# The first three steps of an attention turn: transposes ahead of the first scores on TensorE, bank emptying first on VectorE

## The chip, the cores and the metric

The kernel runs on one core of a Trainium2 chip, in one launch. The metric is the device time of that launch in microseconds (us), lower being better; a comparison takes the median of several runs. One further execution was recorded by the hardware profiler, and all rows below are from it.

## The reference

One transformer layer on an input of 2 sequences, 1024 tokens, 512 features, all in float32:

```python
q = (x @ Wq.T)                       # 32 heads of 128, rotary embedding applied
c_kv = x @ Wdk.T                     # latent of 512
k = mix(rope(x @ Wkr.T), c_kv @ Wupk.T)   # 8 key heads
v = c_kv @ Wupv.T                    # 8 value heads
scores = where(causal, q @ k.T / sqrt(128), -1e9)
out = softmax(scores) @ v            # every key head serves 4 query heads
x = layernorm(x + out @ Wo.T)
x = layernorm(x + W2 @ (silu(W1 @ x) * (W3 @ x)))   # W1, W2, W3 unpacked from 4 bits
```

## The kernel before

**Precision.** Each float32 operand of a large product is split into a rounded part HI and a remainder LO, and each product is made as three matmuls, HI·HI, HI·LO and LO·HI (`three_pass`, L255). So every tile that leaves TensorE and enters a product again is first copied by ScalarE (the HI part) and then subtracted by VectorE (the LO part).

**Stages.** Stage A makes latents, keys and values of all tokens (the first scores start at 232.8 us of the trace). Then come 16 turns of attention, one for each pair of a sequence and a key head (`turn_of`, called by `turns` at L404: a first turn, a loop of turns 1 to 14, a last turn 15, and a short tail called "end"). The feed-forward stage follows. The change touches the turns alone.

**A turn** has 32 steps. A step is one cell: 128 queries (tile i = c // 4) of one query head (h = c % 4) against the keys that they may see. Cells are pipelined over the steps:

- step s: TensorE makes the scores of cell s (`scores`, L1047, into `b_sps`); VectorE takes mask and maximum (`mask_max`, L902) and ScalarE the exponential with its sum (`exp`, L742).
- step s+2: VectorE takes the reciprocal of the sum (`reciprocal`, L911), ScalarE multiplies by it (`normalise`, L749).
- step s+3 (`LAG`): TensorE transposes the weights, in one or two pieces of up to four 128x128 tiles (`transposes`, L1062, into `b_tps`); ScalarE copies a piece to HI (`hi_pt`, L755), VectorE makes LO (`lo_pt`, L916).

Between these TensorE works off a queue of "fill" products by a table (`FILL`, `ROOM`): query projections of a coming half (`q0`, `q1`), weights times values (`pv`), and the output projection (`wo`). A fill product that is finished in step s is taken from its bank by ScalarE and VectorE in step s+1 (`take`): for a query `swap_q` (L715) and `cos_q` (L884), for a `pv` `hi_ot` (L771) and `lo_ot` (L927), for a `wo` `add_y` (L932). One step later still come the second half of the rotary embedding (`add_q`, L891, VectorE), its HI part (`hi_q`, L722, ScalarE) and its LO part (`split_q`, GpSimd).

**What sets the order.** Every engine runs its own list, in order. Within a step the order of the jobs is a tuple of `ACT_ORDER`, `DVE_ORDER` or `PE_ORDER`, the first tuple in steps 0 to 2 (`part_of`, L94). In step 0 TensorE first does all fill of that step, in the loop the 21 matmuls of `pv` tile 6 of the turn before. ScalarE's order in steps 0 to 2, not changed, is: take, first piece, q, normalise, second piece, exp.

**At a turn's start** the three pipelines overlap. Step 0 holds: scores of cell 0 of the new turn, transposes of cell 29 of the turn before, `reciprocal` and `normalise` of cell 30, `cos_q` of the new turn's fourth query head. Step 1 holds: scores of cell 1, transposes of cell 30, `reciprocal` and `normalise` of cell 31, `hi_ot` and `lo_ot` of `pv` tile 6, `add_q` and `hi_q` of the fourth head, and the first 8 matmuls of `wo` tile 5, which go to the bank that `cos_q` empties. Step 2 transposes cell 31. The new turn's keys come by four DMAs that SyncE issues once the last scores of the turn before are made, since there is one key buffer:

```python
if step == 0 and turn in ("loop", "last"):
    sp.wait_ge(s_done, CELLS * it)
    load_k(it)
```

Of the kernel before, what the change touches and what calls it, by code (L numbers as in the profile page):

```python
# [54 lines left out]
def pieces(c):  # L55

    i = c // GQ
    first = c if i < 4 else 16 + 2 * (c - 16)
    out = [(first, 0, min(4, i + 1))]
    if i >= 4:  # L60
        out.append((first + 1, 4, i - 3))
    return out
# [31 lines left out]
def part_of(step):  # L94

    return (step >= LAG) + (step >= 16) + (step >= 24)
# [6 lines left out]
             ("take", "q", "normalise", 0, "exp", 1, "weights"),  # L103
             ("take", "normalise", 0, "exp", "weights", 1, "q"),
             ("take", "normalise", 0, "exp", "weights", 1, "q"))
DVE_ORDER = (("q", "max", "take", 0, 1),
             ("q", "max", "take", 0, 1),
             ("take", "q", "max", 0, 1),
             ("take", "max", "q", 0, 1))
PE_ORDER = (("scores", "fill", "fill", 0, "fill", 1),  # L110
            ("fill", "scores", 0, "fill", "fill", 1),
            ("scores", "fill", 0, "fill", 1, "fill"),
            ("scores", "fill", 0, "fill", 1, "fill"))
# [59 lines left out]
def plan_of(turn):  # L173
    return FIRST if turn == "first" else LOOP
# [9 lines left out]
def cut(parts, weights):  # L184

    total, shares = sum(b - a for _n, a, b in parts), []
    ends = [round(total * sum(weights[:k]) / sum(weights)) for k in range(len(weights) + 1)]
    for lo, hi in zip(ends, ends[1:]):
        at, share = 0, []
        for place, a, b in parts:  # L190
            x, y = max(lo, at), min(hi, at + b - a)
            if x < y:
                share.append((place, a + x - at, a + y - at))
            at += b - a
        shares.append(share)
    return shares
# [68 lines left out]
def attention(nc, x, xT, wqT, wkrT, wdkT, wupkT, wupvT, woT, cosT, sinT, xs_d, k_d, v_d, y_d):  # L265


    with ExitStack() as ctx:
# [112 lines left out]
        def cell_at(step, it, turn):  # L381

            if step >= 0:
                return (it, step) if turn != "end" and step < CELLS else None
            return (it - 1, step + CELLS) if turn != "first" else None
# [444 lines left out]
        def _(dve):  # L830
# [116 lines left out]
            def turn_of(it, turn):  # L947
                for step in steps_of(turn):
                    here = cell_at(step, it, turn)
                    for job in DVE_ORDER[part_of(step)]:  # L950
                        if job == "take":
# [47 lines left out]
        def _(pe):  # L999
# [47 lines left out]
            def scores(it, c):  # L1047
                i, h = c // GQ, c % GQ
                if c == 0 and type(it) is int and it == 0:
                    pe.wait_ge(a_bank_free, a_count(END, VG + V_LATE - 1) + a_FREE0)  # L1050
                if c == 0:
                    pe.wait_ge(k_in, 64 * (it + 1))
                pe.wait_ge(q_lo, 8 * it + 4 * (i // 4) + h + 1 + QLO0)
                pe.wait_ge(sc_done, CELLS * it + c + 1)
                if c in (16, 17):
                    pe.wait_ge(ot_lo, QT * it + c - 16 + 1)
                q = (i % 4) * P
                for k, (a, b) in enumerate(scores_width(i)):
                    last = three_pass(nc, sps[c % 2][:, 512 * k:512 * k + b - a],
                                      [(lambda p: qs[:, i // 4, h, p, q:q + P], lambda p: kt[:, p, a:b])])  # L1060
                last.then_inc(s_done, 1)

            def transposes(it, c, piece):
                n, j0, nj = piece
                pe.wait_ge(norm_done, CELLS * it + c + 1)
                pe.wait_ge(pt_lo, PIECES * it + n + 1)
                for j in range(nj):
                    last = nc.tensor.transpose(tps[n % 2][:, j], sc[:, c % S_RING, (j0 + j) * P:(j0 + j + 1) * P],  # L1068
                                               ident[:])
                last.then_inc(t_done, 1)  # L1070
# [54 lines left out]
            def fill(it, turn, parts):  # L1125
                for n, a, b in parts:
                    if not valid(n, turn):
                        continue
                    kind, t, g, _s = plan_of(turn).fill[n]
                    bk = plan_of(turn).bank[n]  # L1130
                    if a == 0 and bk < 2 and (before := bank_before(n, turn)):
                        bank_taken(before[0], before[1], it + before[2])
                    elif a == 0 and bk < 2:
                        pe.wait_ge(q_cos, GQ - 1 + n)
                    if kind == "pv":
                        values(it + g, t, bk, a, b)
                    elif kind == "wo":
                        project(it + g, t, bk, a, b)
                    elif kind == "va":
                        late_values(t, bk, a, b)  # L1140
                    else:
                        queries(it + g, int(kind == "q1"), t, bk, a, b)

            def turn_of(it, turn):
                for step in range(CELLS):
                    parts = plan_of(turn).spread[step]
                    here, cell = cell_at(step, it, turn), cell_at(step - LAG, it, turn)
                    if step == 0:
                        fill(it, turn, parts)
                        parts = []  # L1150
                    ts = pieces(cell[1]) if cell else []
                    shares = cut(parts, SHARES[len(ts)])
                    for job in PE_ORDER[part_of(step)]:
                        if job == "scores":
                            if here:
                                scores(*here)
                        elif job == "fill":
                            if shares:
                                fill(it, turn, shares.pop(0))
                        elif job < len(ts):  # L1160
                            transposes(*cell, ts[job])
# [16 lines left out]
            for h in range(GQ):  # L1178
# [3 lines left out]
                if h < V_LATE:  # L1182
                    a_group(END, VG + h, a_values(h))
            turns(pe, turn_of)


# [535 lines left out]
```

## Time and profile before

| | us |
|---|---|
| median of 3 runs | 2485.4 |
| lowest and highest of them | 2484.12 and 2489.93 |
| the profiled execution | 2487.67 |
| its span, first to last instruction | 2485.9 |
| TensorE busy with matmuls in the span | 2408.9 (97%) |
| ScalarE busy | 1597.1 (64%) |
| VectorE busy | 1425.2 (57%) |
| GpSimd busy | 571.6 (23%) |

The profiled execution took 1.8 us more than its span. Its mean granted TensorE clock is 0.991 of the full one. The ends of matmul records are modelled, so that TensorE's real occupation is better read from the distance between starts. L12 is line 12 of the kernel. A row that stands for several instructions tells the first start and the time that all were busy; the bracket tells how long the engine was idle ahead of the first one, and what released it. In rows PE is TensorE, PEld its loading of weights (it runs beside the matmuls), DVE VectorE, ACT ScalarE.

### The profile page before, as it was taken

Reading aid. Unit: us, or ns where it says so; the run is one execution under the profiler, and the core shown is the slowest. Engines: PE = TensorE matmul, PEld = TensorE weight load, DVE = VectorE, ACT = ScalarE, POOL = GpSimd, SP = SyncE. Lnnn points to the kernel's source line nnn. Section 1 sums busy time; section 2 is a strip of 40 time slices with the busy share of each in tenths; the row PEclk is TensorE's granted clock in tenths of the full one; section 3 lists DMA queues with packets and bytes.
Section 4 is the critical chain, followed back from the end, with each engine's and each line's share of the span. In section 5 each row is a group of like instructions: output and inputs, shape, how many; then the busy total and the mean of one; then the engine's idle time right before and its main releaser. Section 6 shows DMA issues by size and latency. Waiting matters only on the chain. (4 is left out here: it accounts for less than half of the span.)

```text
span 2485.9 us, 40420 instructions
## 1 busy us (share of the span) xinstructions
PE 2408.9 (97%) x12028; PEld 1997.4 (80%) x12028; DVE 1425.2 (57%) x3333; ACT 1597.1 (64%) x3213; POOL 571.6 (23%) x445
## 2 busy tenths in 40 slices
PE   8999999999999999999999999999999996899998
PEld 7887888888888888888888888888888875678886
DVE  4334656566666666566666666666666666842332
ACT  4223878787777878787777878787877762332211
POOL 3002313223231323132222313231322202300000
PEclk9999999999999999999999999999999998999999
DMA  7767333324242323233242424232332316520100
GB/s 266 276 217 272 124 98 111 114 93 155 67 155 82 131 82 133 93 110 115 96 156 72 148 80 132 90 124 93 110 122 89 116 42 190 153 78 34 51 34 17
DMA packets 110979, 293.38 MB, mean 118 GB/s; under 512 B 10832, under 2 KB 27728, under 8 KB 101648
## 3 DMA queue, kind: packets, MB, share of 16 engines
q1 hardware_dynamic: 110928, 292.73, 35.4%
q8 instruction: 28, 0.46, 0.1%
q14 instruction: 23, 0.19, 0.0%
HBM read 208.80 MB, written 88.08 MB: 119 GB/s over the span
## 5 line engine op out<-in xcount | busy, mean ns | idle before, releaser
L924 DVE TENSOR_TENSOR b_pt<-b_tps,b_pt 128x512 fp32r<-128x512 f32 (+3 forms) x768 | 427.1, 556 | 370.7 <-ACT b_pt L767 369.6
L752 ACT ACTIVATE b_sc<-b_sc,b_rinv 128x896 f32<-128x896 f32 (+7 forms) x512 | 397.0, 775 | 294.4 <-DVE b_rinv L914 290.9
L260 PE MATMUL b_sps<-b_kt,b_qs 128*128 128x512 f32 (+4 forms) x2304 | 501.8, 344 | 10.2 <-DMA b_kt<-k_d 10.1
L260 PEld LDWEIGHTS b_sps<-b_kt,b_qs 128*128 128x128 f32 x2304 | 403.0, 188 | 72.4 <-issue 18.9
L260 PE MATMUL b_ps<-b_xs,b_wq 128*128 128x512 f32 x1536 | 442.3, 407 | 2.6 <-issue 2.6
L260 PE MATMUL b_ps<-b_pt,b_vt 128*128 128x512 f32 x1584 | 436.4, 402 | 2.5 <-DVE b_ys L935 2.5
L260 PE MATMUL b_ps<-b_wo,b_ot 128*128 128x512 f32 x1536 | 423.7, 406 | 1.8 <-DVE b_ys L935 0.6
L767 ACT ACTIVATE b_pt<-b_tps 128x512 fp32r<-128x512 f32 (+3 forms) x768 | 364.5, 475 | 63.7 <-PE b_tps L1068 63.0
L746 ACT ACTIVATE b_sc<-b_sc,b_nmax 128x896 f32<-128x896 f32 (+7 forms) x512 | 392.7, 767 | 1.0 <-DVE b_nmax L906 1.0
L1068 PE MATMUL b_tps<-b_ident,b_sc 128*128 128x128 f32 x2304 | 377.4, 274 | 8.9 <-DVE b_pt L924 5.7
L906 DVE CUSTOM_DVE_ANT_0 b_sc<-b_sps,b_mask 128x896 f32<-128x896 f32 (+7 forms) x512 | 380.2, 743 | 0.0
L1068 PEld LDWEIGHTS b_tps<-b_ident,b_sc 128*128 128x128 f32 x2304 | 287.7, 140 | 97.3 <-DVE b_pt L924 15.8
L260 PEld LDWEIGHTS b_ps<-b_pt,b_vt 128*128 128x128 f32 x1584 | 285.8, 189 | 50.8 <-DVE b_ys L935 2.9
L260 PEld LDWEIGHTS b_ps<-b_xs,b_wq 128*128 128x128 f32 x1536 | 275.1, 190 | 47.7 <-issue 3.0
L260 PEld LDWEIGHTS b_ps<-b_wo,b_ot 128*128 128x128 f32 x1536 | 270.7, 189 | 48.4 <-DVE b_qf L888 4.1
L598 POOL TENSOR_TENSOR b_sw<-b_sw,b_sin 128x512 f32<-128x512 f32 x128 | 165.5, 1293 | 498.5 <-ACT b_sw L720 498.5
L602 POOL TENSOR_TENSOR b_qs<-b_qf,b_qs 128x512 fp32r<-128x512 f32 x124 | 160.3, 1293 | 482.3 <-ACT b_qs L726 482.3
L914 DVE RECIPROCAL b_rinv<-b_rsum 128x1 f32<-128x1 f32 x512 | 81.1, 158 | 194.5 <-PE b_sps L260 182.9
L888 DVE TENSOR_TENSOR b_qf<-b_ps,b_cos 128x512 f32<-128x512 f32 x128 | 88.5, 691 | 98.2 <-ACT b_sw L720 54.2
L260 PE MATMUL c_a<-c_xs,c_w 128*128 (+3 forms) x528 | 135.3, 407 | 8.4 <-DVE c_hb L1508 4.2
L611 POOL TENSOR_TENSOR b_wo<-b_wraw,b_wo 128x512 fp32r<-128x512 f32 x64 | 83.0, 1297 | 239.7 <-ACT b_wo L740 239.7
L1616 PE MATMUL c_y<-c_w,c_hs 128*128 128x512 f32 (+1 forms) x528 | 129.6, 395 | 7.1 <-DVE c_hs L1514 7.1
(137 smaller groups left out, 2386.9 us busy)
## 6 DMA issues: line engine op xcount, KB each, us to landing
b_xs<-xs_d SPq DMA_DIRECT2D x32, 2048.0 KB, 9.1
b_ys<-y_d SPq DMA_DIRECT2D x128, 256.0 KB, 2.7
y_d<-b_ys SPq DMA_DIRECT2D x128, 256.0 KB, 2.5
k_d<-a_ks SPq DMA_DIRECT2D x32, 512.0 KB, 4.2
v_d<-a_vs SPq DMA_DIRECT2D x32, 512.0 KB, 3.0
b_kt<-k_d SPq DMA_DIRECT2D x64, 256.0 KB, 4.5
b_vt<-v_d SPq DMA_DIRECT2D x16, 1024.0 KB, 4.8
b_wraw<-in_wqT SPq DMA_DIRECT2D x64, 256.0 KB, 2.7
```

The lines of the kernel that those rows point to most:

```text
L260: ins = nc.tensor.matmul(out, *every[n], start=(n == 0), stop=(n == len(every) - 1))
L598: nc.gpsimd.tensor_tensor(sw[:], sw[:], sinq[:, blk * TB:blk * TB + TB], ALU.mult).then_inc(sin_done, 1)
L602: nc.gpsimd.tensor_tensor(qs[:, blk, h, LO], qf[:], qs[:, blk, h, HI], ALU.subtract).then_inc(q_lo, 1)
L611: nc.gpsimd.tensor_tensor(wo[:, h, LO], wraw[:, h % 2], wo[:, h, HI], ALU.subtract).then_inc(w_lo, 1)
L746: nc.scalar.activation(sc[:, slot, 0:w], sc[:, slot, 0:w], ACT.Exp, bias=nmax[:, slot:slot + 1], scale=-1.0, accum_out=rsum[:, slot:slot + ...
L752: nc.scalar.activation(sc[:, slot, 0:w], sc[:, slot, 0:w], ACT.Copy, scale=rinv[:, slot:slot + 1])\
L767: nc.scalar.activation(pt[:, u % PT_UNITS, HI, 0:nj, h * P:(h + 1) * P], tps[n % 2][:, 0:nj], ACT.Copy)\
L888: nc.vector.tensor_tensor(qf[:], banks[bk], cosq[:, blk * TB:blk * TB + TB], ALU.mult)\
L906: nc.vector.tensor_tensor_reduce(out=like_banks(sc[:, slot, 0:w], i), in0=both_banks(sps[c % 2], i), in1=like_banks(mask[:, S - w:S], i), ...
L924: nc.vector.tensor_tensor(pt[:, u, LO, 0:nj, h * P:(h + 1) * P], tps[n % 2][:, 0:nj], pt[:, u, HI, 0:nj, h * P:(h + 1) * P], ALU.subtract) ...
L1068: last = nc.tensor.transpose(tps[n % 2][:, j], sc[:, c % S_RING, (j0 + j) * P:(j0 + j + 1) * P], ident[:])
L1616: last = nc.tensor.matmul(yps[t][:], hs[0:w, f % 2, a, t * P:(t + 1) * P], w2[0:w, b, f], start=(f == 0 and k == 0), stop=(f == FT - 1 and ...
```

## The change

Two edits. In step 0 TensorE makes both pieces of transposes, and then the scores. In steps 0 to 2 VectorE does "take" first, then "q", then "max" (which holds the wait for the scores, the reciprocal of an earlier cell, and mask and maximum).

```diff
-DVE_ORDER = (("q", "max", "take", 0, 1),
+DVE_ORDER = (("take", "q", "max", 0, 1),
              ("q", "max", "take", 0, 1),
              ("take", "q", "max", 0, 1),
              ("take", "max", "q", 0, 1))
...
-                    for job in PE_ORDER[part_of(step)]:
+                    for job in (0, 1, "scores") if step == 0 else PE_ORDER[part_of(step)]:
                         if job == "scores":
                             if here:
                                 scores(*here)
```

The lists of ScalarE, GpSimd and SyncE stay as they are. TensorE's list in the loop, from the 21 fill matmuls of step 0 on (b_sps is written by scores, b_tps by transposes):

```order
 L260 MATMUL b_ps<-b_pt,b_vt 128x512 x21
+L1065 ISA
+L1066 REGISTER_ALU
+L1068 MATMUL b_tps<-b_ident,b_sc 128x128 x4
+L1066 REGISTER_ALU
+L1068 MATMUL b_tps<-b_ident,b_sc 128x128 x4
 L1052 ISA
 L1053 ISA
 L1054 ISA
 L260 MATMUL b_sps<-b_kt,b_qs 128x256 x3
```

The eight transposes of cell 29, with their waits, now stand ahead of the waits and the three matmuls of the first scores; before, they stood behind them.

VectorE's list in the loop, step 0, before (b_qf is `cos_q`, b_rinv the reciprocal, L906 mask and maximum, b_pt `lo_pt`):

```order
L914 RECIPROCAL b_rinv<-b_rsum 128x1
L906 ISA b_sc,b_nmax<-b_sps,b_mask 128x128
L906 ISA b_nmax 128x1
L886 ISA
L888 TENSOR_TENSOR b_qf<-b_ps,b_cos 128x512
L920 ISA
L924 TENSOR_TENSOR b_pt<-b_tps,b_pt 128x4x128
```

and now:

```order
L888 TENSOR_TENSOR b_qf<-b_ps,b_cos 128x512
L899 ISA
L900 ISA
L913 ISA
L914 RECIPROCAL b_rinv<-b_rsum 128x1
L906 ISA b_sc,b_nmax<-b_sps,b_mask 128x128
L906 ISA b_nmax 128x1
L920 ISA
L924 TENSOR_TENSOR b_pt<-b_tps,b_pt 128x4x128
```

`cos_q` moved from behind the maximum to the front, ahead of the wait for the scores (L899).

VectorE's list in the loop, step 1, before (the first b_qf row is `add_q`, b_ot is `lo_ot`):

```order
L895 TENSOR_TENSOR b_qf<-b_qf,b_sw 128x512
L899 REGISTER_ALU
L900 REGISTER_ALU
L913 REGISTER_ALU
L914 RECIPROCAL b_rinv<-b_rsum 128x1
L906 ISA b_sc,b_nmax<-b_sps,b_mask 128x128
L906 ISA b_nmax 128x1
L928 ISA
L929 TENSOR_TENSOR b_ot<-b_ps,b_ot 128x512
```

and now:

```order
L928 ISA
L929 TENSOR_TENSOR b_ot<-b_ps,b_ot 128x512
L895 TENSOR_TENSOR b_qf<-b_qf,b_sw 128x512
L899 REGISTER_ALU
L900 REGISTER_ALU
L913 REGISTER_ALU
L914 RECIPROCAL b_rinv<-b_rsum 128x1
L906 ISA b_sc,b_nmax<-b_sps,b_mask 128x128
L906 ISA b_nmax 128x1
```

`lo_ot`, with its wait for ScalarE's `hi_ot` (L928), moved ahead of `add_q` and of the reciprocal.

## Rows read from the trace of the kernel before

**Rows 1.** The page's part 1: busy time, share of the span and instructions by engine.

```profile
PE 2408.9 (97%) x12028; PEld 1997.4 (80%) x12028; DVE 1425.2 (57%) x3333; ACT 1597.1 (64%) x3213; POOL 571.6 (23%) x445
```

**Rows 2.** TensorE's waits over the whole span: total us, times, longest.

```profile
PE b_sps L260 <- DMA b_kt<-k_d: 10.1, 14, 1.0
...
PE b_tps L1068 <- DVE b_pt L924: 5.7, 20, 0.6
```

**Rows 3.** Timeline of one turn's start, TensorE: start us, us, engine line op [idle before <-releaser].

```profile
452.74 4.94 PE L260 MATMUL b_ps<-b_pt,b_vt 128*128 128x512 f32 x21
...
458.27 0.61 PE L260 MATMUL b_sps<-b_kt,b_qs 128*128 128x256 f32 x3 [0.59 <-DMA b_kt<-k_d]
...
458.72 1.04 PE L1068 MATMUL b_tps<-b_ident,b_sc 128*128 128x128 f32 x8
...
459.52 0.60 PE L260 MATMUL b_sps<-b_kt,b_qs 128*128 128x256 f32 x3
...
460.20 1.24 PEld L260 LDWEIGHTS b_ps<-b_wo,b_ot 128*128 128x128 f32 x6 [0.29 <-DVE b_qf L888]
...
461.73 0.60 PE L1068 MATMUL b_tps<-b_ident,b_sc 128*128 128x128 f32 x4
...
464.64 0.51 PEld L1068 LDWEIGHTS b_tps<-b_ident,b_sc 128*128 128x128 f32 x4
464.79 0.60 PE L1068 MATMUL b_tps<-b_ident,b_sc 128*128 128x128 f32 x4
```

**Rows 4.** The same timeline, ScalarE.

```profile
459.36 0.60 ACT L767 ACTIVATE b_pt<-b_tps 128x512 fp32r<-128x512 f32 x1 [3.62 <-PE b_tps L1068]
...
459.86 1.14 ACT L752 ACTIVATE b_sc<-b_sc,b_rinv 128x1024 f32<-128x1024 f32 x1
...
460.90 0.59 ACT L767 ACTIVATE b_pt<-b_tps 128x512 fp32r<-128x512 f32 x1
...
461.76 0.59 ACT L774 ACTIVATE b_ot<-b_ps 128x512 fp32r<-128x512 f32 x1
...
462.36 0.60 ACT L767 ACTIVATE b_pt<-b_tps 128x512 fp32r<-128x512 f32 x1
...
462.86 0.62 ACT L726 ACTIVATE b_qs<-b_qf 128x512 fp32r<-128x512 f32 x1
...
463.38 1.14 ACT L752 ACTIVATE b_sc<-b_sc,b_rinv 128x1024 f32<-128x1024 f32 x1
```

**Rows 5.** The same timeline, VectorE.

```profile
459.13 0.16 DVE L914 RECIPROCAL b_rinv<-b_rsum 128x1 f32<-128x1 f32 x1 [3.91 <-PE b_sps L260]
...
461.52 0.69 DVE L924 TENSOR_TENSOR b_pt<-b_tps,b_pt 128x512 fp32r<-128x512 f32 x1 [0.77 <-ACT b_pt L767]
...
462.12 0.68 DVE L895 TENSOR_TENSOR b_qf<-b_qf,b_sw 128x512 f32<-128x512 f32 x1
...
462.72 0.15 DVE L914 RECIPROCAL b_rinv<-b_rsum 128x1 f32<-128x1 f32 x1
...
462.99 0.68 DVE L929 TENSOR_TENSOR b_ot<-b_ps,b_ot 128x512 fp32r<-128x512 f32 x1
```

**Rows 6.** The same timeline, two pairs of a releaser and an idle ScalarE.

```profile
451.06 0.16 DVE L914 RECIPROCAL b_rinv<-b_rsum 128x1 f32<-128x1 f32 x1
...
451.26 1.15 ACT L752 ACTIVATE b_sc<-b_sc,b_rinv 128x1024 f32<-128x1024 f32 x1 [1.04 <-DVE b_rinv L914]
...
472.96 0.69 DVE L895 TENSOR_TENSOR b_qf<-b_qf,b_sw 128x512 f32<-128x512 f32 x1 [0.48 <-POOL b_sw L598]
...
473.68 0.63 ACT L726 ACTIVATE b_qs<-b_qf 128x512 fp32r<-128x512 f32 x1 [1.05 <-DVE b_qf L895]
```

**Rows 7.** Timeline of the last turn's start, TensorE.

```profile
1933.79 1.52 PE L260 MATMUL b_ps<-b_pt,b_vt 128*128 128x512 f32 x6
...
1935.39 0.62 PE L260 MATMUL b_sps<-b_kt,b_qs 128*128 128x256 f32 x3
```

**Rows 8.** Timeline behind the last turn, TensorE alone.

```profile
2045.00 0.63 PE L1068 MATMUL b_tps<-b_ident,b_sc 128*128 128x128 f32 x4 [0.50 <-DVE b_pt L924]
```

## Prediction

> **What bounds the kernel now.** I read the page's busy shares first: TensorE 97%, no other engine over 64% [rows 1]. So time can only be won where TensorE stands still, or lost by making it stand still. Next TensorE's waits. The largest entry inside the attention turns is the first scores of a turn waiting for the keys: 10.1 us in 14 waits, 0.72 us each, one in each of the 14 turns of the loop; the second is transposes waiting for VectorE's `lo_pt`, 5.7 us in 20 [rows 2]. Then the timeline of one turn's start on three engines. TensorE starts its 21 fill matmuls at 452.74. They cost 0.2275 us each (the row's 4.94 less the modelled 0.39 of the last, over 20), so TensorE is free at 457.52; the first scores start at 458.27, when the keys are there, and the transposes that the keys have nothing to do with stand behind them, from 458.72 [rows 3]. A second small wait follows: the six `wo` matmuls start at 460.20, their weights having waited 0.29 for `cos_q`, which stood behind the maximum [rows 3]. The reader is to see one more thing: ScalarE is idle for 3.62 us before 459.36 and then has ten or so operations without a gap up to `normalise` at 463.38 [rows 4], and the transposes of step 2 at 464.79 need the result of that one [rows 3].
>
> **What goes away.** The eight transposes take 458.72 to 459.52, 0.80 us, and 0.80 is more than the 0.75 between 457.52 and 458.27 [rows 3]. So they start at 457.52, the scores at about 458.31 instead of 458.27, the second scores (0.44 later) at 458.75 instead of 459.52. `cos_q` now runs in VectorE's idle 3.91 us [rows 5]: what it needs from ScalarE was done by 455.74, which is 459.36 less 3.62 [rows 4]. The `wo` matmuls can then start when the second scores are issued, at 459.10 instead of 460.20: TensorE is 1.1 us ahead there. If that lasted, 15 turns by 1.1 would be 16.5 us.
>
> **What it costs: the chain that the scores start.** In step 0 VectorE's reciprocal of cell 30 stands behind the wait for the scores, in both kernels, and ScalarE's list hangs on it. The scores come 0.04 later, so nothing behind them on that path comes earlier by TensorE's 1.1 us. I follow it with distances between starts.
>
> 1. Reciprocal of cell 30: 458.27 to 459.13 is 0.86 [rows 3, 5]; now 458.31 + 0.86 = 459.17.
> 2. `normalise` of cell 30: an idle ScalarE starts 0.20 behind a reciprocal (451.06, 451.26) [rows 6]; now 459.37. Before 459.86, because ScalarE was at the first piece's copy from 459.36 [rows 4]; that copy now comes over a microsecond sooner. This is all that ScalarE wins: 0.49.
> 3. Copy of the second piece 1.04 later, at 460.41, `hi_ot` 0.86 after that, at 461.27 (before 460.90 and 461.76) [rows 4].
> 4. VectorE: the second `lo_pt` at 460.41 + 0.62 = 461.03 (before 460.90 to 461.52 [rows 4, 5]), free again 0.60 later at 461.63. Then comes the moved `lo_ot`, which waits for `hi_ot`: with the same 0.62, 461.89. It stood at 462.99 before, when its input had been ready for long [rows 5].
> 5. `add_q` is now behind it: 461.89 + 0.60 = 462.49, before 462.12 [rows 5]. The wait for `hi_ot` is thus added in front of `add_q`, and behind `add_q` in VectorE's queue are the reciprocal of cell 31, the second maximum and the next `lo_pt`; only the first matters, since it goes from 462.72 to 463.09, still ahead of its use.
> 6. `hi_q`: 0.72 after `add_q` with ScalarE idle (472.96, 473.68) [rows 6]: 463.21, before 462.86, when ScalarE reached it straight from the copy at 462.36 [rows 4]. ScalarE now stands idle there.
> 7. `normalise` of cell 31: 0.52 later, 463.73, before 463.38. It lasts 1.14 [rows 4], so it ends at 464.87 instead of 464.52, and the weights of the step 2 transposes are loaded 0.12 after (before: 464.64) [rows 3], at 464.99.
> 8. TensorE pays for a restart after a wait. The six `wo` matmuls, which had waited, take 1.53 to the next start, 460.20 to 461.73, against 6 x 0.2275 = 1.37: 0.16 [rows 3]. Transposes are not shown restarting, so their price lies between 0 and 0.16; loads and matmuls of theirs are half as long, and I take 0.05. The transposes run at 465.04 instead of 464.79.
>
> So in a turn of the loop TensorE is 1.1 us ahead at the `wo` matmuls and 0.25 us behind at the transposes of step 2. Its own work would have brought it there at 459.10 + (464.79 - 460.20) = 463.69; it gives back about 0.2 at the transposes of cell 30 (loaded at 459.37 + 1.14 + 0.12 = 460.63, where TensorE would be at 459.10 + 1.37 = 460.47), another 0.2 at their second piece, which waits for the `lo_pt` at 461.03, and some 0.9 at step 2. What follows in the turn hangs on TensorE and on the same chain, and is late by the same quarter of a microsecond; the next turn's keys are asked for after the last scores, so nothing gives it back.
>
> **The sum.**
> - 14 turns of the loop, 0.25 each: 3.5 us. Bounds: 0.15 and 0.45 (step 8 at 0 and each of the eight steps a hundredth shorter; step 8 at 0.16 and half of that again at the second piece, whose `lo_pt` hangs on the same `normalise`).
> - Turns whose keys come earlier than here: the scores then wait for the transposes instead. The mean wait is 0.72, here it is 0.59 by the page's count; that costs at most 0.15 where it is shorter, and I take 0.3 us for all, between 0 and 1.
> - The last turn: the fill ends at 1933.79 + 6 x 0.2275 = 1935.15 and the scores start at 1935.39 [rows 7], 0.24 later and not 0.75. The transposes' 0.80 moves them by 0.55, and the chain behind moves along: 0.7, between 0.4 and 0.9.
> - Behind the last turn there are no scores, but `lo_ot` stands ahead of the last reciprocal, by one distance of 0.60 [rows 5]; the transposes there already wait 0.50 for VectorE [rows 8], so the chain decides there too. 0.6, between 0 and 0.6.
> - The first turn makes no transposes in step 0; the emptied bank ahead of the maximum delays one exponential, which step 3's transposes use much later: 0, between -0.3 and 0.3.
> - Instructions added or removed: none of any weight. No DMA moves past another.
>
> Together 3.5 + 0.3 + 0.7 + 0.6 = 5.1 us: from the profiled execution's 2487.67 to 2492.8. That execution lies 2.3 above the median of the three runs, 2485.4; from the median I get 2490.5, 0.2% slower. A measurement of this kernel tells about 0.3%, 7.5 us, from no change, so most of this counts as the same.
>
> One rule speaks against my result. The row shows a wait of 0.59 for the keys ahead of work that does not need them [rows 3]. The Trainium skill, DMA: Bandwidth & Descriptors, section Rules for kernel authors, says to issue a DMA early, do compute, and wait on its semaphore late; by it the 10.1 us of [rows 2] would be the gain. The trace agrees that the wait can be covered, not that its end is what decides step 2.
>
> **Rivals.**
> - *The wait's removal shows in the time (faster).* If `hi_q` or the `normalise` behind it can run when they did before, TensorE keeps at least the wait: 10.1 us, to 2475.3, and with the `cos_q` wait up to 16.5, to 2469. For it: the largest wait inside the turns goes. Against: step 5, where `add_q` has an input that did not exist before, and step 2, by which ScalarE gets only 0.49. Chance 0.13.
> - *The chain's cost is paid more than once (slower).* Three groups of transposes hang on the late `normalise`: step 2's first, its second, and cell 0's in step 3. In the forecast the second and third are late with the first. If a restart costs the full 0.16, the first pays 0.11 more than I took; and if one more of them restarts from a wait of its own, another 0.11. A turn then costs 0.25 + 2 x 0.11 = 0.47, so 6.6 + 1.6 = 8.2 us: 2493.6, over the bound. It decides once the second piece's `lo_pt` ends later than TensorE gets to it; by the distances above it ends at 463.73 + 1.04 + 0.62 + 0.69 = 466.08, within 0.1 of that point. For it: the transposes already wait for `lo_pt` 20 times [rows 2]. Against: those waits are 0.28 on average. With the last turn and the keys at their ends it reaches 2497. Chance 0.20.
> - *The order does not do what it says.* If TensorE cannot start the transposes at 457.52, because the bank pair or the weights of cell 29 are late, nothing moves on TensorE, and the late scores stay. Their weights were normalised from 451.26 on [rows 6], six microseconds before. Then 0 to +2 us, 2486. Chance 0.05, within the same.
>
> **How the numbers follow.** Forecast 0.62, faster rival 0.13, slower rival 0.20, no effect 0.05. Faster by over 0.3%: 0.13; slower by over 0.3%: 0.20 (the slower rival's part over the bound, and a little of the forecast's upper end in exchange for its lower part); same: 0.67. The likeliest case alone spans 2487 to 2493. The range is 2478 to 2496: it leaves out most of the faster rival and the last of the slower one.
>
> **What would show it.** Right: the wait for the keys gone from TensorE's list or under 2 us; the first scores of a turn still about 0.2 us behind the keys' landing; in its place about 14 waits of transposes for ScalarE's `normalise`, 0.7 to 1.1 us each, some 13 us; VectorE's `add_q` 4.2 us after the turn's first scores instead of 3.85; ScalarE idle ahead of `hi_q`; step 2's transposes 6.7 us after those scores instead of 6.52. Wrong: if those transposes come 6.5 us or less after the first scores, the chain of steps 4 to 7 was shorter than I have it, and the time falls below 2485; if TensorE's sum of waits grows by over 10 us, the slower rival holds.

## The result, and the profile after

| | before | changed |
|---|---|---|
| median of 18 runs each, us | 2487.41 | 2493.59 |
| lowest and highest | 2482.83, 2491.27 | 2486.35, 2496.09 |
| span of the profiled execution | 2485.9 | 2492.1 |

The ratio is 1.0024, with a 95% interval of 1.0017 to 1.0031: 4.2 to 7.7 us slower, clear of zero and within what I had called the same. Forecast were +5.1 us. One run of the kernel before, among those that e5 to e7 below are held against, took 2976.7 us at a granted clock of 0.749 instead of 0.99 and is left out of every figure.

The page's first line shows nothing of it: TensorE is busy to the same 97% as in [rows 1].

```profile
PE 2415.9 (97%) x12028; PEld 1995.6 (80%) x12028; DVE 1427.4 (57%) x3333; ACT 1599.1 (64%) x3213; POOL 571.9 (23%) x445
```

TensorE's waits over the span show where the time went (total us, times, longest). They answer to [rows 2].

```profile
PE b_tps L1068 <- ACT b_sc L752: 15.1, 30, 0.9
...
PE b_tps L1068 <- DVE b_pt L924: 5.7, 19, 0.6
...
PE b_sps L260 <- DMA b_kt<-k_d: 1.2, 3, 0.6
```

The wait for the keys is down from 10.1 us to 1.2, as intended. The keys have not lost their say, though: in 11 of the loop's 14 turns the scores still start 0.21 to 0.22 us behind the landing of the last key transfer, as before; what is gone is the idle time ahead of them, now filled with transposes. In its place stand transposes that wait for ScalarE's `normalise`, 15.1 us; before, that pair had 1.2 us in 8.

The start of the loop's third turn in the changed kernel, TensorE, in the columns of [rows 3]:

```profile
572.04 1.04 PE L1068 MATMUL b_tps<-b_ident,b_sc 128*128 128x128 f32 x8
...
573.08 0.97 PE L260 MATMUL b_sps<-b_kt,b_qs 128*128 128x256 f32 x6
...
573.89 1.55 PE L260 MATMUL b_ps<-b_wo,b_ot 128*128 128x512 f32 x6
...
575.42 0.65 PE L1068 MATMUL b_tps<-b_ident,b_sc 128*128 128x128 f32 x4
...
576.55 0.66 PE L1068 MATMUL b_tps<-b_ident,b_sc 128*128 128x128 f32 x4
...
579.79 0.42 PEld L1068 LDWEIGHTS b_tps<-b_ident,b_sc 128*128 128x128 f32 x4 [1.27 <-DVE b_pt L924]
579.80 0.65 PE L1068 MATMUL b_tps<-b_ident,b_sc 128*128 128x128 f32 x4 [0.86 <-ACT b_sc L752]
```

The transposes come first, the scores follow at 573.08 without idle time ahead of them, and the six `wo` matmuls start 0.81 behind the scores instead of 1.93. Then every group of transposes in steps 1 and 2 restarts from a wait (in the trace the loads of their weights stood idle 0.41, 0.44, 1.27 and 0.22 ahead of the four groups), and the first of step 2, at 579.80, has waited 0.86. It starts 6.72 behind the first scores; before it was 464.79 - 458.27 = 6.52 [rows 3].

ScalarE in the same stretch, to be held against [rows 4]:

```profile
572.68 0.60 ACT L767 ACTIVATE b_pt<-b_tps 128x512 fp32r<-128x512 f32 x1 [2.42 <-PE b_tps L1068]
...
574.14 1.15 ACT L752 ACTIVATE b_sc<-b_sc,b_rinv 128x1024 f32<-128x1024 f32 x1 [0.87 <-DVE b_rinv L914]
...
576.06 0.58 ACT L774 ACTIVATE b_ot<-b_ps 128x512 fp32r<-128x512 f32 x1
...
578.00 0.63 ACT L726 ACTIVATE b_qs<-b_qf 128x512 fp32r<-128x512 f32 x1 [0.87 <-DVE b_qf L895]
...
578.54 1.13 ACT L752 ACTIVATE b_sc<-b_sc,b_rinv 128x1024 f32<-128x1024 f32 x1
```

Its first copy comes early and then it is idle, first 0.87 for the reciprocal, later 0.87 for `add_q`. Before, it had no gap between these operations. VectorE, against [rows 5]:

```profile
573.95 0.16 DVE L914 RECIPROCAL b_rinv<-b_rsum 128x1 f32<-128x1 f32 x1 [2.96 <-PE b_sps L260]
...
576.67 0.69 DVE L929 TENSOR_TENSOR b_ot<-b_ps,b_ot 128x512 fp32r<-128x512 f32 x1 [0.18 <-ACT b_ot L774]
...
577.28 0.68 DVE L895 TENSOR_TENSOR b_qf<-b_qf,b_sw 128x512 f32<-128x512 f32 x1
...
577.88 0.16 DVE L914 RECIPROCAL b_rinv<-b_rsum 128x1 f32<-128x1 f32 x1
```

`lo_ot` waits for `hi_ot` (idle 0.18), and `add_q` comes at 577.28, 4.20 behind the first scores; before, 462.12 - 458.27 = 3.85.

The period of a turn splits into three parts. These are means over the 14 turns of the loop, from the starts in the two traces, in us:

| | before | changed | difference |
|---|---|---|---|
| keys asked for, until the first scores | 7.106 | 7.231 | +0.125 |
| of that, until the keys have landed | 6.887 | 6.997 | +0.110 |
| first scores, until the transposes of step 2 | 6.514 | 6.715 | +0.201 |
| those transposes, until the next keys are asked for | 100.030 | 100.041 | +0.011 |
| a whole turn | 113.649 | 113.987 | +0.338 |

14 x 0.338 = 4.7 of the spans' 6.2 us. The second line is the transfer itself; in the seven other kernels below its mean lay between 6.79 and 6.96 whatever they changed, and here three of the 14 turns (7.65, 7.37 and 7.35, the others 6.64 to 7.05) make the 7.00. So I take its 0.11 (1.5 us in the sum) for scatter of one execution; with one trace of each kernel that is not shown. The granted clock was 1.00 from 260 to 1929 us in both traces, so it has no part in the turns' difference. In the last turn the scores come 0.56 and the transposes another 0.12 later. The first turn, from its first scores to the request for the next keys, is 0.08 shorter, 104.53 instead of 104.61. Behind the last turn, in the changed kernel (TensorE):

```profile
2043.95 1.03 PE L1068 MATMUL b_tps<-b_ident,b_sc 128*128 128x128 f32 x8
...
2050.63 0.63 PE L1068 MATMUL b_tps<-b_ident,b_sc 128*128 128x128 f32 x4 [0.64 <-DVE b_pt L924]
2053.27 3.35 PE L260 MATMUL b_ps<-b_pt,b_vt 128*128 128x512 f32 x7 [2.01 <-DVE b_ys L935]
```

and before:

```profile
2038.87 1.03 PE L1068 MATMUL b_tps<-b_ident,b_sc 128*128 128x128 f32 x8
...
2047.63 1.67 PE L260 MATMUL b_ps<-b_pt,b_vt 128*128 128x512 f32 x6 [2.01 <-DVE b_ys L935]
```

From the first transposes to the restart of the `pv` matmuls it is 9.32 instead of 8.76, 0.56 longer. These parts make 5.9 of the 6.2 us; the rest, under 0.4, lies in stages that the change does not touch.

### The profile page after: what moved, and what is told of

Same layout as the page of the kernel before. It is cut to its first block and busy times, and to the rows that moved or that the text cites. A ratio compares the mean times of both kernels' runs of the same rounds, so it can differ in the third digit from the quotient of the medians.

```text
span 2492.1 us, 40420 instructions
## 1 busy us (share of the span) xinstructions
PE 2415.9 (97%) x12028; PEld 1995.6 (80%) x12028; DVE 1427.4 (57%) x3333; ACT 1599.1 (64%) x3213; POOL 571.9 (23%) x445
## 5 line engine op out<-in xcount | busy, mean ns | idle before, releaser
L260 PE MATMUL b_ps<-b_pt,b_vt 128*128 128x512 f32 x1584 | 437.8, 404 | 2.5 <-DVE b_ys L935 2.5
L1068 PE MATMUL b_tps<-b_ident,b_sc 128*128 128x128 f32 x2304 | 379.8, 275 | 22.0 <-ACT b_sc L752 15.1
L906 DVE CUSTOM_DVE_ANT_0 b_sc<-b_sps,b_mask 128x896 f32<-128x896 f32 (+7 forms) x512 | 380.4, 743 | 0.0
```

The lines of the kernel that those rows point to most:

```text
L260: ins = nc.tensor.matmul(out, *every[n], start=(n == 0), stop=(n == len(every) - 1))
L906: nc.vector.tensor_tensor_reduce(out=like_banks(sc[:, slot, 0:w], i), in0=both_banks(sps[c % 2], i), in1=like_banks(mask[:, S - w:S], i), ...
```

## Experiments

All seven were compared with the kernel before. The first four shared 15 runs of it (median 2486.88), the last three 27 (median 2485.91). The distances in the text are from the third turn, those in the table means over the 14 turns of the loop. The turns tell more than the whole times, since stages that no edit touches vary from trace to trace: the first scores start at 231.1 to 233.8 us, and from the restart of `pv` behind the last turn to the end it is 437.8 to 440.8.

| | scores to `add_q` | to `normalise` of cell 31 | to step 2's transposes | a turn | ratio to before, 95% |
|---|---|---|---|---|---|
| before | 3.85 | 5.10 | 6.51 | 113.65 | |
| changed | 4.20 | 5.45 | 6.72 | 113.99 | 1.0024 (1.0017 to 1.0031) |
| e1 TensorE's order alone | 3.33 | 5.07 | 6.50 | 113.55 | 0.9995 (0.9986 to 1.0004) |
| e2 VectorE's order alone | 4.72 | 5.97 | 7.23 | 114.22 | 1.0039 (1.0025 to 1.0052) |
| e3 take first in step 0 only | 3.33 | 4.59 | 5.90 | 112.95 | 0.9965 (0.9952 to 0.9979) |
| e4 e3 and early reciprocal | 2.53 | 3.86 | 5.38 | 112.41 | 0.9932 (0.9919 to 0.9946) |
| e5 changed and early reciprocal | 3.42 | 4.67 | 5.99 | 112.98 | 0.9975 (0.9966 to 0.9984) |
| e6 e4 with TensorE's old order | 3.86 | 5.11 | 6.38 | 113.50 | 0.9995 (0.9987 to 1.0004) |
| e7 e3, `lo_ot` behind `add_q` | 3.33 | 4.72 | 6.00 | 113.04 | 0.9977 (0.9968 to 0.9985) |

**e1.** The second hunk of the change alone; `DVE_ORDER` as before.

```diff
-                    for job in PE_ORDER[part_of(step)]:
+                    for job in (0, 1, "scores") if step == 0 else PE_ORDER[part_of(step)]:
```

> TensorE's half of the change alone: transposes ahead of the first scores in step 0, VectorE's order as before. Theory (the chain add_q, hi_q, normalise of cell 31 decides step 2, and only the moved lo_ot makes it late): the wait for the keys goes from TensorE's list, but the 0.7 to 0.9 us come back as a wait of the wo matmuls for cos_q, which still stands behind the maximum. add_q stays about 3.4 to 3.9 us and step 2's transposes about 6.5 us behind the turn's first scores. Time: +0.04 us a turn and 0.6 in the last turn, 0 to +2 us, same. Rival (making the scores wait behind the transposes is what costs): step 2's transposes 6.7 us behind the scores, +4 to +6 us. Third (the wait for the keys was the price): -10 us.

Measured: 2486.43 us against 2486.88, no difference. TensorE, third turn:

```profile
571.86 0.97 PE L260 MATMUL b_sps<-b_kt,b_qs 128*128 128x256 f32 x6
...
573.79 1.66 PE L260 MATMUL b_ps<-b_wo,b_ot 128*128 128x512 f32 x6 [0.96 <-DVE b_qf L888]
...
578.39 0.60 PE L1068 MATMUL b_tps<-b_ident,b_sc 128*128 128x128 f32 x4
```

The wait for the keys is gone and stands again, somewhat longer (14.1 us in 15 waits over the span), in front of the `wo` matmuls, released by `cos_q` behind the maximum. The transposes of step 2 start 6.53 behind the scores. So the transposes' precedence alone neither costs nor gains.

**e2.** The first hunk alone.

```diff
-DVE_ORDER = (("q", "max", "take", 0, 1),
+DVE_ORDER = (("take", "q", "max", 0, 1),
```

> VectorE's half alone: take, q, max in steps 0 to 2, TensorE's order as before. Theory: hi_ot comes only at 3.49 us behind the first scores as before, lo_ot 0.62 later, add_q at 4.71 (before 3.85), hi_q 5.43, normalise of cell 31 at 5.95 (before 5.10), step 2's transposes at 7.25 instead of 6.51: +0.74 us a turn, with 0.6 in the last turn and 0.6 behind it +11.5 us, 0.4 to 0.5 percent slower. Rival (the emptying of the bank for wo is what matters, the 0.29 us wait goes): -4 us. Rival (TensorE's order carries the loss): 0.

Measured: 2496.95 us, ratio 1.0039, 6 to 13 us slower. TensorE's scores, VectorE's `add_q`, TensorE's transposes of step 2:

```profile
572.66 0.62 PE L260 MATMUL b_sps<-b_kt,b_qs 128*128 128x256 f32 x3 [1.12 <-DMA b_kt<-k_d]
...
577.38 0.68 DVE L895 TENSOR_TENSOR b_qf<-b_qf,b_sw 128x512 f32<-128x512 f32 x1
...
579.90 0.65 PE L1068 MATMUL b_tps<-b_ident,b_sc 128*128 128x128 f32 x4 [0.84 <-ACT b_sc L752]
```

4.72 and 7.24 where 4.71 and 7.25 were expected. By the turns VectorE's new order alone costs more than the whole change, 7.23 against 6.72 from scores to transposes: the two hunks work against each other. The medians go the same way, but the intervals of the two ratios overlap.

**e3.** Both engines as changed in step 0, VectorE as before in steps 1 and 2 (`DVE_ORDER` not edited).

```diff
-                    for job in DVE_ORDER[part_of(step)]:
+                    for job in ("take", "q", "max", 0, 1) if step == 0 else DVE_ORDER[part_of(step)]:
...
-                    for job in PE_ORDER[part_of(step)]:
+                    for job in (0, 1, "scores") if step == 0 else PE_ORDER[part_of(step)]:
```

> The change as it is in step 0 on both engines, but VectorE's steps 1 and 2 in the order of before (q, max, take), so that add_q no longer waits behind lo_ot. Theory: add_q 3.3 us behind the first scores instead of 4.2, normalise of cell 31 at 4.6, step 2's transposes 5.9 us behind the first scores: 0.6 us a turn faster than before, -8 us against before and -14 against the changed kernel. Rival (the late scores or the landing of the keys carry the loss, not lo_ot): no faster than before, +3 to +6 us.

Measured: 2477.81 us, ratio 0.9965: about 9 us faster than before. The same three points:

```profile
567.76 0.96 PE L260 MATMUL b_sps<-b_kt,b_qs 128*128 128x256 f32 x6
...
571.08 0.68 DVE L895 TENSOR_TENSOR b_qf<-b_qf,b_sw 128x512 f32<-128x512 f32 x1
...
573.61 0.66 PE L1068 MATMUL b_tps<-b_ident,b_sc 128*128 128x128 f32 x4
```

3.32 and 5.85. The only difference to the changed kernel in the loop is where `lo_ot` stands in step 1 (in step 2 nothing is taken), and it turns 6 us lost into 9 won. The rival (late scores or late keys carry the loss) falls: the scores stand behind the transposes as in the changed kernel, and the keys, which landed after 6.82 us in the mean instead of 7.00, make at most 0.17 of the 1.03 us that a turn is shorter.

**e4.** e3, and in step 0 the reciprocal ahead of the wait for the scores.

```diff
+                            cell = cell_at(step - 2, it, turn)
+                            if cell and step == 0:
+                                reciprocal(*cell)
                             if here:
                                 scores_there(*here)
-                            if cell := cell_at(step - 2, it, turn):
+                            if cell and step > 0:
                                 reciprocal(*cell)
                             elif here:
                                 nc.vector.memset(spare[:, step:step + 1], 0.0)
```

> As the kernel with take first in step 0 only, and in step 0 the reciprocal of cell 30 also stands ahead of VectorE's wait for the scores (a tiny memset takes that wait). Theory: ScalarE's normalise of cell 30 no longer hangs on the scores, the whole list of ScalarE starts about 0.7 us earlier, and TensorE keeps the whole 1.1 us of a turn: step 2's transposes 5.4 us behind the first scores, -15 us against before (2472 to 2474). Rival (VectorE's wait for the scores is not on the path, TensorE's own work is): same time as without this edit.

Measured: 2469.84 us, ratio 0.9932, 17 us faster than before; no kernel here is faster. Scores, ScalarE's `normalise` of cell 30, `add_q`, transposes of step 2:

```profile
568.22 0.97 PE L260 MATMUL b_sps<-b_kt,b_qs 128*128 128x256 f32 x6
568.55 1.15 ACT L752 ACTIVATE b_sc<-b_sc,b_rinv 128x1024 f32<-128x1024 f32 x1
...
570.82 0.68 DVE L895 TENSOR_TENSOR b_qf<-b_qf,b_sw 128x512 f32<-128x512 f32 x1
...
573.49 0.60 PE L1071 MATMUL b_tps<-b_ident,b_sc 128*128 128x128 f32 x4
```

`normalise` of cell 30 starts 0.33 behind the scores instead of 1.06, and the transposes of step 2 follow the matmuls before them without a wait, 5.27 behind the scores. That is TensorE's own work: the chain is off the path. Twelve of the 14 turns have 5.25 to 5.30. In the other two a different wait shows, that for the DMA of the next block's inputs (`b_xs`), which delays the query products ahead of those transposes: in the first turn TensorE waits 0.95 us for it and the transposes come at 6.48, in the fourth at 5.50. In e3 it is the first turn alone (0.57 us of waiting, 6.57; the others 5.84 to 5.87). The means of the table, 5.38 and 5.90, contain these turns. The first turn of e4, whose scores start at 342.56:

```profile
348.48 0.73 PE L260 MATMUL b_ps<-b_xs,b_wq 128*128 128x512 f32 x2 [0.95 <-DMA b_xs<-xs_d]
...
349.04 0.60 PE L1071 MATMUL b_tps<-b_ident,b_sc 128*128 128x128 f32 x4
```

**e5.** The changed kernel with e4's edit of the reciprocal.

> The changed kernel, lo_ot still ahead of add_q, and in step 0 the reciprocal of cell 30 ahead of VectorE's wait for the scores. Theory (the chain that lo_ot lengthens starts at the scores only because the reciprocal hangs on them): ScalarE's normalise, hi_ot and so lo_ot come 0.7 us earlier, add_q 3.5 us behind the first scores instead of 4.2, step 2's transposes 6.0 instead of 6.7: 0.7 us a turn better than the changed kernel, -4 to -6 us against before. Rival (lo_ot costs by its place alone, wherever ScalarE is): as the changed kernel, +6.

Measured: 2480.12 us, ratio 0.9975, 6 us faster than before and some 12 faster than the changed kernel.

```profile
571.59 0.96 PE L260 MATMUL b_sps<-b_kt,b_qs 128*128 128x256 f32 x6
...
575.06 0.68 DVE L895 TENSOR_TENSOR b_qf<-b_qf,b_sw 128x512 f32<-128x512 f32 x1
...
577.58 0.65 PE L1071 MATMUL b_tps<-b_ident,b_sc 128*128 128x128 f32 x4 [0.58 <-ACT b_sc L752]
```

`add_q` still comes behind `lo_ot`, now 3.47 behind the scores, the transposes 5.99. The price of `lo_ot`'s place depends on when ScalarE gets to `hi_ot`, which is what the theory says. Against e4, whose order differs by `lo_ot`'s place, it still costs 0.61 us a turn in the means, and 0.66 without the turns that wait for `b_xs` (here the first, with 1.18 us of waiting and 6.71 from scores to transposes). The 14 turns of the trace are 9.4 us shorter than before, more than the 6 of the whole time; behind the last turn 0.56 is lost as in the changed kernel, and the stages that no edit touches took 3.4 us longer in this trace.

**e6.** e4 without the hunk on TensorE's order.

> VectorE as in the kernel with the early reciprocal and take first in step 0 only, TensorE's order as before. Theory: with the transposes behind the scores ScalarE's first copy of the turn comes at 459.4 as before, so the early reciprocal is of no use, and TensorE keeps its wait for the keys; only the 0.29 us wait of the wo matmuls goes, and step 2's transposes then wait a little for normalise: -0.1 us a turn, 0 to -3 us. Rival (the early reciprocal and the early cos_q carry the 17 us that the kernel with both orders won): -10 us or more.

Measured: 2484.93 us, ratio 0.9995, no difference that can be told. The mean distance to step 2's transposes fell by 0.14 as expected, 2 us in the sum. Early reciprocal and early `cos_q` are worth almost nothing as long as the transposes stand behind the scores.

**e7.** e3 with `lo_ot` behind `add_q` but ahead of the reciprocal of cell 31.

```diff
-DVE_ORDER = (("q", "max", "take", 0, 1),
+DVE_ORDER = (("q", "take", "max", 0, 1),
```

> As the kernel with take first in step 0 only, but in steps 1 and 2 VectorE's order is q, take, max: lo_ot behind add_q and still ahead of the reciprocal of cell 31. Theory (add_q is what lo_ot must not delay; the reciprocal has 0.4 us to spare): add_q 3.3 us and step 2's transposes 5.9 us behind the first scores, as without this edit, -7.5 to -8.5 us against before (0.6 lost behind the last turn). Rival (the reciprocal of cell 31 is the link that decides): step 2's transposes 6.3 us or more, -3 us or worse.

Measured: 2480.46 us, ratio 0.9977, 5.7 us faster where 7.5 to 8.5 were expected. `add_q`, `lo_ot`, the reciprocal, `normalise` of cell 31:

```profile
571.70 0.68 DVE L895 TENSOR_TENSOR b_qf<-b_qf,b_sw 128x512 f32<-128x512 f32 x1
...
572.30 0.68 DVE L929 TENSOR_TENSOR b_ot<-b_ps,b_ot 128x512 fp32r<-128x512 f32 x1
...
572.90 0.15 DVE L914 RECIPROCAL b_rinv<-b_rsum 128x1 f32<-128x1 f32 x1
...
573.08 1.15 ACT L752 ACTIVATE b_sc<-b_sc,b_rinv 128x1024 f32<-128x1024 f32 x1
```

Neither theory met it whole. `add_q` is where it was in e3, and most of the gain stands, so `add_q` is the main link. But the reciprocal, 0.60 later, now releases `normalise` (0.18 ahead of it), 0.13 later than in e3. In e3 it starts 0.66 ahead of `normalise`, of which 0.20 is the way to ScalarE: 0.46 to spare, near the 0.4 that I had given it, and `lo_ot` takes 0.60. I had the spare time right and did not subtract. That explains 0.13 us a turn, under 2 us, and not the whole shortfall: the 14 turns of the trace are 8.5 us shorter than before, about what 0.6 a turn would give, 0.4 and 0.56 are lost in the last turn and behind it, and the execution of the kernel before that was traced lay 1.8 above the median of the 27, so that against the median there is less to gain.

## Why the prediction was right

It was right in direction, size and place; the terms, one by one:

- **What goes away.** TensorE's lead at the `wo` matmuls, 1.1 us forecast: 1.12 in the third turn, from 1.93 to 0.81 behind the scores. The wait for the keys fell to 1.2 us.
- **Steps 1 to 4.** From the scores: reciprocal 0.87 (forecast 0.86), `normalise` of cell 30 1.06 (1.06), `hi_ot` 2.98 (2.96), `lo_ot` 3.59 (3.58).
- **Steps 5 to 7.** `add_q` 4.20 (4.18), `hi_q` 4.92 (4.90), `normalise` of cell 31 5.46 (5.42). e3 shows that this part is the cause and not a companion, e2 that it does the same without TensorE's hunk, e5 that it starts where the reciprocal hangs on the scores.
- **Step 8.** The load of the waited-for transposes starts at 6.71 (forecast 6.68). The restart was guessed at 0.05; the four transposes take 0.65 instead of 0.60, which is that. The matmul starts 0.20 later than before, with the restart 0.25.
- **The sum.** The loop's term was 3.5; measured is 14 x (0.201 + 0.011) = 3.0, the rest of the restart included, and 1.5 more from keys that landed later in this one execution. Scores waiting for transposes: forecast 0.3, measured 14 x (0.125 - 0.110) = 0.2. The last turn: 0.7, measured 0.56 + 0.12 = 0.7. Behind the last turn: 0.6, measured 0.56. The first turn: forecast 0, measured -0.08. Without the keys' 1.5 these give 4.4 against a forecast of 5.1 and a median difference of 6.2, within its interval of 4.2 to 7.7. In the two traces the keys and the untouched stages fill the gap of 1.8; that they do so in the medians is not shown.
- **The time itself.** Measured were 2493.59, forecast 2490.5 from the median of three runs, with 2487 to 2493 for the likeliest case alone. Two of the three us between are the starting point, since 18 runs of the kernel before have a median of 2487.41 and not 2485.4. That the slower rival had named 2493.6 is chance: without the keys' 0.11 a turn grew by 0.23, which is near the forecast's 0.25 and not its 0.47.
- **The rivals.** The faster one fails in e1: the wait can be removed at no gain, since the next wait on the same engine takes its place. The slower one had part of its mechanism: the second piece of step 2 does wait (its weights' load starts at 580.93, behind `lo_pt`, by the trace), but its matmuls start 1.18 behind those of the first piece, before 1.14 (means of the 14 turns), and that is the 0.05 of the first piece's restart; the scores behind them follow within 0.01 of the distance of before, so it adds nothing like 0.11. The third, that nothing moves on TensorE, falls with the transposes at 572.04, ahead of the keys' landing at 572.87.
- **The signs named.** The waits of transposes for `normalise` came as 15.1 us in 30 instead of some 13 in 14. Of these, 15 waits with 12.7 us are the ones forecast, at step 2 of the loop's turns and the last; 14 with 2.2 us stand some 46 us into the turns, where the kernel before had 8 with 1.2, and one of 0.2 behind the last turn. The scores are on average 0.23 behind the landing. TensorE's waits within the loop grew from 15.1 to 19.0 us, far from the 10 that would have spoken for the slower rival.

What the prediction did not see is that the change was one line from a gain. It priced the chain, and stopped where it could have asked which link was free to move.

## What to carry to other kernels

When a stall of the busiest engine is covered by reordering, follow every other engine's list from the same event to its next meeting with that engine; the gain is the smallest of what the lists give, and here ScalarE's gave half a microsecond and then lost it. In an in-order queue, put ahead what others wait for, and not what itself waits for the slowest neighbour: the same `lo_ot` cost 0.8 us a turn when it stood ahead of `add_q` (6.72 against 5.90). And two reorderings that are each worth nothing (e1, e6) can be worth 17 us together (e4), so they are to be tried as a set, chosen by the chain.

## What the runs showed of the hardware

A group of transposes that had waited cost about 0.05 us more than one that had not (0.65 against 0.60 for four), a group of six 512-column matmuls 0.11 to 0.16 (a record of 1.66 in e1, where they had waited, against 1.55 in the changed kernel; 1.53 between starts against 6 x 0.2275 in the third group of rows). The four key transfers, always of the same size and issued behind the same event, took between 6.79 and 7.00 us in the mean of 14 turns in the nine kernels, one execution each; over 14 turns that is an estimated 3 us of time where the scores start behind their landing.
